# Scores of all four row groups together, and a new order within a tick, in block 0 of a two-block transformer kernel

## The chip, the cores and the metric

The kernel runs on one core of a Trainium2 chip. The metric is the device time of one execution in microseconds. Five engines work from instruction queues of their own, each strictly in order, and meet at semaphores: TensorE (PE, with its weight loads listed apart as PEld), VectorE (DVE), ScalarE (ACT), GpSimd (POOL) and SyncE (SP, which issues transfers here).

## What is computed

Two transformer blocks work on x of 64 batches x 128 tokens x 256 channels, with a context of 64 x 128 x 192 and a conditioning vector. The part that matters here is block 0, whose attention has 16 heads of only 16 channels:

```
def _attn(q, k, v):          # 16 heads of 16 channels
    scores = jnp.einsum('bhnd,bhmd->bhnm', q, k) * HD ** (-0.5)
    p = jax.nn.softmax(scores, axis=-1)
    o = jnp.einsum('bhnm,bhmd->bhnd', p, v)
    return o.transpose(0, 2, 1, 3).reshape(o.shape[0], o.shape[2], D)
h = _ln(x, ln1_w, ln1_b) * (1 + sc1[:, None, :]) + sh1[:, None, :]
qkv = h @ Wqkv + bqkv
x = x + _attn(q, k, v) @ Wos + bos                                     # pass 0
h = _ln(x, ln2_w, ln2_b) * (1 + sc2[:, None, :]) + sh2[:, None, :]
x = x + _attn(h @ Wq + bq, context @ Wk + bk, context @ Wv + bv) @ Woc + boc   # pass 1
```

A feed-forward (pass 2) and block 1 (passes 3 to 5: self attention with 16 heads of 64 channels, cross attention, feed-forward) follow.

## The kernel before

**Work and ticks.** Six passes over the data, each in 16 groups of four batches. `schedule()` writes out by hand, for every stage of every batch, the tick in which it is issued; every engine's program walks the ticks and issues, within a tick, the stages in one fixed order. In passes 0 and 1 ("block 0" in the change's name and here: self and cross attention of the first block, KIND "a") a group takes 16 ticks and a batch four: batch b of a group starts at `tb = tg + 4*b`. Below, "tick 0 to 3" is the tick within a batch's four. The engines aren't synchronised by ticks; a tick is only an order of issue.

**One batch, pass 0 or 1.** fp32 operands are split into a high part (rounded to fp32r) and a low part (the rest), and a product takes three fp32r matmuls (high x high, high x low, low x high; `three`, L607 to L609). q and k are projected for a group of four batches in two units j = 0, 1 each: `q` and `k` on PE (the k projection has a bias matmul more, L709), then `q_high`/`k_high` on ACT (L879; L887, L888) and `q_low`/`k_low` on DVE (L1088; L1095, two operations). The 16 heads lie in four row groups of 32 partitions: row group r serves PSUM bank r (PS[0] to PS[3]), with four heads in each bank.

- `scores0` (PE, L687): in halves. Half h makes banks 2h and 2h+1, as six steps of two matmuls, one in each of two row groups. Half 0 of batch B is issued at tick 2 of batch B-1, half 1 at tick 0 of B.
- `max0` (DVE, L1050): negated maximum of a half's two banks, one tick after its scores.
- `exp0` (ACT, L904): tile u (bank u, four heads), at tick u: four activations with accumulated sums.
- `normal`: reciprocal on DVE (L1063) and product on POOL (L1234), tick u+1.
- `p_turn` (PE, L801): four transposes of the tile, tick u+3. `p_copy` of it out of PSUM, tick u+4: DVE for u < 3 (L1058), ACT for u = 3 (L940).
- `pv0` (PE, L734): probabilities times v, tick 8, that is tick 0 of the batch two later. `high0` (ACT, L895, writes OH) and `low0` (DVE, L1102, writes OL) at tick 9. `out0` (PE, L607 to L609 with OH and OL), tick 10. `res0` (DVE, L1083), tick 11.
- `v` (PE) at tick -3, `v_out` (DVE, L1074) at tick -2.

For a coming group the kernel computes statistics (DVE), normalises (POOL, L1277), turns (`turn`, PE, L823, four parts in four ticks that fall into batch 2 of the current group) and modulates (`hf`, ACT, L951), then splits (`split`, DVE L1010 and POOL L1239). Pass 1 has turns of the context too (`c_turn`, L834), their copies (`c_hf`), splits (`c_split`) and `c_merge` on DVE, on which the k and v projections of that pass wait.

**Order within a tick.** PE: scores0, q, k, v, pv0, out0, p_turn, turn, c_turn. ACT: q_high, k_high, high0, exp0, p_copy, hf, c_hf. DVE: max0, p_copy, normal, v_out, res0, q_low, k_low, low0, statistics, split, c_split, c_merge. POOL: normal, split, c_split, root, norm, bias.

**PSUM.** Banks 0 to 3 hold the scores. Banks 4 to 7 (FOUR) are handed out in turn by `Banks.add`, in the order in which the uses are issued on PE: every projection, v, pv, out0 result, turned tile and turn takes the next of the four and waits until the use four back has been read. A batch without turns has eight uses: pv, p, v, p, out0, p, q or k, p.

The scores wait for the banks at L683: `q.wait_ge(s_exp, 4 * (4 * ga + x.b) + 2 * x.h - 2)`, that is: half 0 waits for the exponentials of tiles 0 and 1 of the batch before, half 1 for tiles 2 and 3.

Of the kernel before, what the change touches and what calls it, by code (L numbers as in the profile page):

```python
# [8 lines left out]
ACT = mybir.ActivationFunctionType  # L9
# [4 lines left out]
NG = NB // G  # L14
# [112 lines left out]
def schedule():  # L127
# [3 lines left out]
    for p, kind in enumerate(KIND):  # L131
        for g in range(NG):
# [51 lines left out]
            if kind == "a":  # L184
                for j in range(2):
                    tq, tk = (tg - 17 + 4 * j, tg - 9 + 4 * j) if (p, g) != (0, 0) else (tg - 17 + j, tg - 15 + j)
                    tq += 2 * ((p, g) == (0, 1))
                    at["q", tq].append((p, g, j))
                    at["q_high", tq + 1].append((p, g, j))
                    at["q_low", tq + 1].append((p, g, j))  # L190
                    at["k", tk].append((p, g, j))
                    at["k_high", tk + 1].append((p, g, j))
                    at["k_low", tk + 1].append((p, g, j))
# [15 lines left out]
            for b in range(G):  # L209
                tb = tg + 4 * b  # L210
                for h in range(2):
                    at["scores0", tb + 2 * h - 2].append(Half(2 * (4 * (NG * p + g) + b) + h, p, g, b, h))
                    at["max0", tb + 2 * h - 1].append(Half(2 * (4 * (NG * p + g) + b) + h, p, g, b, h))
                for stage, tick in (("v", tb - 3), ("v_out", tb - 2), ("pv0", tb + 8), ("high0", tb + 9), ("low0", tb + 9),
                                    ("out0", tb + 10), ("res0", tb + 11)):
                    at[stage, tick].append(Batch(p, g, b))
                for u in range(4):
                    t = Tile(n, p, ATT[p], g, b, u)
                    for stage, lag in (("exp0", 0), ("normal", 1), ("p_turn", 3), ("p_copy", 4)):
                        at[stage, tb + u + lag].append(t)  # L220
                    n += 1
# [19 lines left out]
def build(nc, a, out):  # L241
    ctx = ExitStack()
    with ctx:
# [118 lines left out]
        def xq(p, g):  # L362
            return NG * p + g
# [63 lines left out]
        for tick in ticks:  # L427
            if tick == TM:
                tp.add("modulation", (7,), s_mod, 3)
            for p, g, j in at["q", tick]:  # L430
                tp.add(("q", p, g, j), FOUR, s_al, 2 * xq(p, g) + j + 1)
            for p, g, j in at["k", tick]:
                tp.add(("k", p, g, j), FOUR, s_kbl, 2 * xq(p, g) + j + 1)
# [17 lines left out]
            for t in at["p_turn", tick]:  # L451
                tp.add(("p", t.n), FOUR if t.n < NL0 else THREE, *pt_done(t))
            for stage in ("turn", "c_turn"):
# [146 lines left out]
        def _(e):  # L600
# [66 lines left out]
            for tick in ticks:  # L667
# [8 lines left out]
                for x in at["scores0", tick]:  # L676
# [5 lines left out]
                    q.wait_ge(s_exp, 4 * (4 * ga + x.b) + 2 * x.h - 2)  # L682
                    for c in range(2):  # L683
                        for k, (qt, kt) in enumerate(((AH, KBH), (AH, KBL), (AL, KBH))):
                            for r in (2 * x.h, 2 * x.h + 1):
# [3 lines left out]
                    made.then_inc(s_s0, 1)  # L689

                for p, g, j in at["q", tick]:
                    u, h = h_of(p, g)
                    key = "Wq" if p == 1 else "Wqkv"
                    q.wait_ge(s_hl, 2 * u + 2)
                    q.wait_ge(s_wlo, w_ready[key])
                    q.wait_ge(*tp.free(("q", p, g, j)))
                    project_t(key, 128 * j, h, PS[tp.bank(("q", p, g, j))]).then_inc(s_q, 1)

                for p, g, j in at["k", tick]:
                    u, h = h_of(p, g, p == 1)  # L700
                    key, col0 = ("Wk", 0) if p == 1 else ("Wqkv", 256)
                    q.wait_ge(s_hl, 2 * u + 2)
                    q.wait_ge(s_wlo, w_ready[key])
                    q.wait_ge(s_bk, 2)
                    if p == 1:
                        q.wait_ge(s_hm, cq(p, g) + 1)
                    q.wait_ge(*tp.free(("k", p, g, j)))
                    bank = PS[tp.bank(("k", p, g, j))]
                    e.matmul(bank[:, :], BK[:, p, 128 * j:128 * j + 128], ONES[:, :], start=True, stop=False)  # L709
                    project_t(key, col0 + 128 * j, h, bank, False).then_inc(s_k, 1)  # L710
# [92 lines left out]

                for x in at["out", tick]:
# [57 lines left out]
        def _(e):  # L862
# [9 lines left out]

            for tick in ticks:
                for p, g, j in at["q_high", tick]:
# [21 lines left out]

                for t in at["exp0", tick]:
                    q.wait_ge(s_nm0, t.n // 2 + 1)
                    q.wait_ge(s_t, t.n - NP0 + 1)
                    q.wait_ge(s_nrm, t.n - NP0 + 1)  # L900
                    bank, pr, nm = PS[t.u], PR[npr(t)[0]], NM0[t.n // 2 % 3][:, 4 * (t.n % 2):4 * (t.n % 2) + 4]
                    for h in range(4):
                        r = slice(128 * h, 128 * h + 128)
                        made = e.activation(pr[:, r], bank[:, r], ACT.Exp, bias=nm[:, h:h + 1], accum_out=RL[npr(t)[0]][:, h:h + 1])  # L904
                    made.then_inc(s_exp, 1)
# [59 lines left out]
                for p, g, j in at["up", tick]:  # L965
# [4 lines left out]
                    e.activation(GF[p][f % 3][:, :], PS[tp.bank(("up", p, g, j))][:, :], ACT.Gelu, bias=col(WFF[p][2], j)).then_inc(s_gf, 1)  # L970

# [357 lines left out]
```

## Time and profile before

| | us |
|---|---|
| median of 3 runs (lowest, highest) | 4212.19 (4211.66, 4212.67) |
| the profiled execution, its own time | 4212.79 |
| its span in the profile | 4210.6 |
| PE busy / ACT / DVE / POOL (share of the span) | 4066.8 (97%) / 2751.7 (65%) / 2858.3 (68%) / 2903.7 (69%) |
| L904 exponentials of block 0, 2048 of them | 730.8, and 516.8 for reading their sums |

Times in the trace are microseconds from the span's start, one execution. A group of instructions is named by its line, engine, operation and tiles (written <- read), its shape and count; "idle before" is the time in which that engine had nothing to run ahead of the instruction, with the engine and line that ended the wait. Two starts subtracted give the time that the earlier instruction takes in a queue; the duration in a row is longer where the next one overlaps it. PEclk is the clock that TensorE was granted, 1.00 being 2.4 GHz and 0.50 the lower level.

### The profile page before, as it was taken

The numbers are of one execution on the slowest core, as the hardware profiler recorded it, in microseconds if no ns is written. First come the engines' busy times: TensorE is split into PE (matmuls) and PEld (weight loads), VectorE is DVE, ScalarE is ACT, GpSimd is POOL, SyncE is SP. The second block draws the span as 40 slices with busy tenths as digits, with TensorE's granted clock in tenths as the row PEclk, the third lists the DMA queues.
The fourth block names the chain that finished last, engine by engine and source line by source line (L and its number), as shares of the span: only waits on it lengthen the run. The fifth ranks groups of instructions, "written<-read, shape, count | busy, mean of one in ns | idle before, by whom it ended". The sixth has DMA issues, their size and how long they took to land.

```text
span 4210.6 us, 95756 instructions
## 1 busy us (share of the span) xinstructions
PE 4066.8 (97%) x34870; PEld 3478.2 (83%) x34870; DVE 2858.3 (68%) x6066; ACT 2751.7 (65%) x10788; POOL 2903.7 (69%) x2706
## 2 busy tenths in 40 slices
PE   7999999999999999999999999999999999999999
PEld 6777777777779988888888888888888888888998
DVE  7888888888865556565656565777776767664443
ACT  6999999999953336666666666666666666665333
POOL 5777788888767775666665665666666666666776
PEclk9999999999999999999999999999999999999999
DMA  2101111111111122212121212322222222221110
GB/s 83 32 32 32 32 45 39 43 47 47 50 54 46 61 63 78 82 70 81 71 81 70 80 71 96 105 78 90 85 83 87 83 86 81 89 98 55 41 51 31
DMA packets 230900, 276.64 MB, mean 66 GB/s; under 512 B 38044, under 2 KB 160416, under 8 KB 230432
## 3 DMA queue, kind: packets, MB, share of 16 engines
q1 hardware_dynamic: 230364, 270.51, 19.1%
q8 instruction: 278, 4.55, 0.5%
q14 instruction: 190, 1.56, 0.1%
q10 hardware_dynamic: 68, 0.02, 0.0%
HBM read 85.89 MB, written 50.33 MB: 32 GB/s over the span
## 4 chain that ended last, share of the span: by engine, by line
PE 76%; POOL 9%; DVE 7%; ACT 4%; issue 3%; DMA 0%; ACTq 0%; SPq 0%; DVEq 0%; POOLq 0%
PE BANKS L607 18%; PE BANKS L609 16%; PE BANKS L608 16%; PE BANKS L801 7%; PE BANKS L765 6%; PE BANKS L753 6%; POOL PR L1234 3%; PE BANKS L687 2%; ACT PR L904 2%; POOL Z L1277 2%; PE BANKS L823 2%; POOL HL L1244 1%; DVE WL L1095 1%; POOL X L1291 1%; DVE PT L1058 1%
## 5 line engine op out<-in xcount | busy, mean ns | idle before, releaser
L1234 POOL TENSOR_TENSOR PR<-PR,RL 128x512 f32<-128x512 f32 x1024 | 1067.8, 1047 | 657.7 <-DVE RL L1063 655.8
L920 ACT ACTIVATE PR<-BANKS,NM 128x128 f32<-128x128 f32 x2048 | 730.6, 382 | 443.6 <-DVE NM L1109 439.2
L904 ACT ACTIVATE PR<-BANKS,NM 128x128 f32<-128x128 f32 x2048 | 730.8, 412 | 12.5 <-DVE NM L1050 10.4
L607 PE MATMUL BANKS<-HH,WH 128*128 128x512 f32 x1632 | 689.0, 422 | 5.3 <-POOL HL L1239 2.7
L801 PE MATMUL BANKS<-ID,PR 128*128 128x128 f32 x4096 | 623.7, 275 | 59.3 <-POOL PR L1234 23.5
L1109 DVE TENSOR_REDUCE NM<-BANKS 128x8 f32<-128x1024 f32 x256 | 313.4, 1224 | 488.0 <-PE BANKS L765 488.0
L608 PE MATMUL BANKS<-HL,WH 128*128 128x512 f32 x1632 | 642.6, 394 | 0.0
L609 PE MATMUL BANKS<-HH,WL 128*128 128x512 f32 x1632 | 641.6, 393 | 0.0
L801 PEld LDWEIGHTS BANKS<-ID,PR 128*128 128x128 f32 x4096 | 487.3, 140 | 184.3 <-POOL PR L1234 66.5
L904 ACT ACTIVATION_READ_ACCUMULATOR PR<-BANKS,NM 128x1 f32 x2048 | 516.8, 253 | 0.0
L920 ACT ACTIVATION_READ_ACCUMULATOR PR<-BANKS,NM 128x1 f32 x2048 | 452.6, 221 | 0.0
L1239 POOL TENSOR_TENSOR HL<-HF,HH 128x512 fp32r<-128x512 f32 x192 | 255.4, 1331 | 232.7 <-DVE HH L1011 218.6
L940 ACT ACTIVATE PT<-BANKS 128x512 f32<-128x512 f32 x640 | 405.4, 634 | 10.6 <-PE BANKS L801 1.5
L607 PE MATMUL BANKS<-WH,OH 128*128 128x256 f32 x1280 | 393.6, 307 | 5.7 <-DVE OL L1102 4.7
L607 PEld LDWEIGHTS BANKS<-HH,WH 128*128 128x128 f32 x1632 | 307.1, 188 | 106.8 <-DVE SN L1123 26.4
L951 ACT ACTIVATE HF<-BANKS,MODB,MODS 128x128 f32<-128x128 f32 x768 | 304.2, 482 | 118.8 <-PE BANKS L823 108.0
L1058 DVE COPY PT<-BANKS 128x512 f32<-128x512 f32 x384 | 263.9, 687 | 150.6 <-PE BANKS L801 149.6
L609 PEld LDWEIGHTS BANKS<-HH,WL 128*128 128x128 f32 x1632 | 307.4, 188 | 70.8
L609 PE MATMUL BANKS<-WH,OL 128*128 128x256 f32 x1280 | 358.0, 280 | 0.0
L608 PE MATMUL BANKS<-WL,OH 128*128 128x256 f32 x1280 | 357.3, 279 | 0.0
L911 ACT ACTIVATE OH<-BANKS 128x512 fp32r<-128x512 f32 x256 | 153.6, 600 | 301.2 <-PE BANKS L753 300.7
L1123 DVE TENSOR_TENSOR SN<-BANKS,ROPE 128x512 f32<-128x512 f32 x512 | 348.8, 681 | 1.6 <-DMA SW<-SN 1.5
(132 smaller groups left out, 10742.0 us busy)
## 6 DMA issues: line engine op xcount, KB each, us to landing
SW<-SN SPq DMA_DIRECT2D x1024, 128.0 KB, 2.1
x_scratch<-X SPq DMA_DIRECT2D x80, 512.0 KB, 3.1
X<-x_scratch SPq DMA_DIRECT2D x80, 512.0 KB, 4.0
CX<-in_ctx SPq DMA_DIRECT2D x32, 384.0 KB, 4.1
X<-in_x SPq DMA_DIRECT2D x16, 512.0 KB, 3.8
out<-X SPq DMA_DIRECT2D x16, 512.0 KB, 2.9
CX<-in_ctx SPq DMA_DIRECT2D x32, 128.0 KB, 4.3
STG<-in_L_xcond_W SPq DMA_DIRECT2D x4, 512.0 KB, 4.9
```

The source lines that it names most:

```text
L607: e.matmul(o, lh, rh, start=first and i == 0, stop=False)
L608: e.matmul(o, lh, rl, start=False, stop=False)
L609: made = e.matmul(o, ll, rh, start=False, stop=last and i == n - 1)
L801: made = e.transpose(bank[:, 128 * h:128 * h + 128], PR[npr(t)[0]][:, 128 * h:128 * h + 128], ID[:, :])
L904: made = e.activation(pr[:, r], bank[:, r], ACT.Exp, bias=nm[:, h:h + 1], accum_out=RL[npr(t)[0]][:, h:h + 1])
L920: made = e.activation(pr[:, r], bank[:, r], ACT.Exp, bias=nm[:, h:h + 1], accum_out=RL[npr(t)[0]][:, h:h + 1])
L940: e.activation(PT[npt(t)[0]][:, :], PS[tp.bank(("p", t.n))][:, :], ACT.Copy).then_inc(s_pt_a, 1)
L951: made = e.activation(HF[u % 2][:, x.c, r], bank[:, r], ACT.Identity, bias=MODB[:, s, x.c, bb:bb + 1], scale=MODS[:, s, x.c, bb:bb + 1])
L1058: e.tensor_copy(PT[npt(t)[0]][:, :], PS[tp.bank(("p", t.n))][:, :]).then_inc(s_pt_d, 1)
L1109: e.tensor_reduce(NM[x.i % 2][:, :], BANKS[:, 2:4, :].rearrange("p e (h k) -> p (e h) k", h=4), AX, ALU.max, negate=True).then_inc(s_nm, 1)
L1123: e.tensor_tensor(SN[r % 2][:, :].rearrange("p (b t) -> p b t", b=G), src, sn, ALU.mult).then_inc(s_rt, 1)
L1234: e.tensor_tensor(p3, p3, RL[npr(t)[0]][:, :].unsqueeze(2).broadcast_to([128, 4, 128]), ALU.mult).then_inc(s_nrm, 1)
```

## The change

1. Scores of a batch are made in one go: one PE stage at tick 0 of the batch, six steps of four matmuls, one in each row group. It waits for all exponentials of the batch before.
2. The maxima of its halves are at ticks 0 and 1 (they were at -1 and 1).
3. The q and k projections are issued one tick earlier (tick 2 in place of tick 3) and stand behind p_turn in the tick, for PE and for the order of the banks; the high parts are a tick earlier too (tick 3), the low parts stay where they were (tick 0).
4. On ACT, the exponentials of tiles 1, 2 and 3 are first in their tick, that of tile 0 is last in its tick, behind the modulation copies.

The diff, cut only where a moved piece stands twice:

```diff
--- before.py
+++ after.py
@@ -183,14 +183,14 @@
                 continue
             if kind == "a":
                 for j in range(2):
-                    tq, tk = (tg - 17 + 4 * j, tg - 9 + 4 * j) if (p, g) != (0, 0) else (tg - 17 + j, tg - 15 + j)
-                    tq += 2 * ((p, g) == (0, 1))
+                    tq, tk, late = (tg - 18 + 4 * j, tg - 10 + 4 * j, 2) if (p, g) != (0, 0) else (tg - 17 + j, tg - 15 + j, 1)
+                    tq += 4 * ((p, g) == (0, 1))
                     at["q", tq].append((p, g, j))
                     at["q_high", tq + 1].append((p, g, j))
-                    at["q_low", tq + 1].append((p, g, j))
+                    at["q_low", tq + late].append((p, g, j))
                     at["k", tk].append((p, g, j))
                     at["k_high", tk + 1].append((p, g, j))
-                    at["k_low", tk + 1].append((p, g, j))
+                    at["k_low", tk + late].append((p, g, j))
             if kind == "b":
                 for j in range(8):
                     x = Unit(unit, p, g, j)
@@ -208,9 +208,9 @@
                 continue
             for b in range(G):
                 tb = tg + 4 * b
+                at["scores0", tb].append(Batch(p, g, b))
                 for h in range(2):
-                    at["scores0", tb + 2 * h - 2].append(Half(2 * (4 * (NG * p + g) + b) + h, p, g, b, h))
-                    at["max0", tb + 2 * h - 1].append(Half(2 * (4 * (NG * p + g) + b) + h, p, g, b, h))
+                    at["max0", tb + h].append(Half(2 * (4 * (NG * p + g) + b) + h, p, g, b, h))
                 for stage, tick in (("v", tb - 3), ("v_out", tb - 2), ("pv0", tb + 8), ("high0", tb + 9), ("low0", tb + 9),
                                     ("out0", tb + 10), ("res0", tb + 11)):
                     at[stage, tick].append(Batch(p, g, b))
@@ -427,10 +427,6 @@
         for tick in ticks:
             if tick == TM:
                 tp.add("modulation", (7,), s_mod, 3)
-            for p, g, j in at["q", tick]:
-                tp.add(("q", p, g, j), FOUR, s_al, 2 * xq(p, g) + j + 1)
-            for p, g, j in at["k", tick]:
-                tp.add(("k", p, g, j), FOUR, s_kbl, 2 * xq(p, g) + j + 1)
             for x in at["v", tick]:
                 tp.add(("v", x), FOUR, s_vd, 4 * xq(x.p, x.g) + x.b + 1)
             for x in at["pv0", tick]:
@@ -450,6 +446,10 @@
                 tp.add(("k1", x.i), THREE if x.i > 1 else TWO, s_rt, 2 * x.i + 2)
             for t in at["p_turn", tick]:
                 tp.add(("p", t.n), FOUR if t.n < NL0 else THREE, *pt_done(t))
+            for p, g, j in at["q", tick]:
+                tp.add(("q", p, g, j), FOUR, s_al, 2 * xq(p, g) + j + 1)
+            for p, g, j in at["k", tick]:
+                tp.add(("k", p, g, j), FOUR, s_kbl, 2 * xq(p, g) + j + 1)
             for stage in ("turn", "c_turn"):
                 for x in at[stage, tick]:
                     hparts[stage, x] = len(hparts)
@@ -679,35 +679,14 @@
                     q.wait_ge(s_mod, 2)
                     q.wait_ge(s_al, 2 * ga + 2)
                     q.wait_ge(s_kbl, 2 * ga + 2)
-                    q.wait_ge(s_exp, 4 * (4 * ga + x.b) + 2 * x.h - 2)
+                    q.wait_ge(s_exp, 4 * (4 * ga + x.b))
                     for c in range(2):
                         for k, (qt, kt) in enumerate(((AH, KBH), (AH, KBL), (AL, KBH))):
-                            for r in (2 * x.h, 2 * x.h + 1):
+                            for r in range(4):
                                 rows = slice(32 * r, 32 * r + 32)
                                 made = e.matmul(PS[r][:, 256 * c:256 * c + 256].rearrange("p (e n) -> p e n", e=2), qt[ga % 2][rows, c, s],
                                                 kt[ga % 2][rows, c, :, s], start=k == 0, stop=k == 2)
-                    made.then_inc(s_s0, 1)
-
-                for p, g, j in at["q", tick]:
-                    u, h = h_of(p, g)
-                    key = "Wq" if p == 1 else "Wqkv"
-                    q.wait_ge(s_hl, 2 * u + 2)
-                    q.wait_ge(s_wlo, w_ready[key])
-                    q.wait_ge(*tp.free(("q", p, g, j)))
-                    project_t(key, 128 * j, h, PS[tp.bank(("q", p, g, j))]).then_inc(s_q, 1)
-
-                for p, g, j in at["k", tick]:
-                    u, h = h_of(p, g, p == 1)
-                    key, col0 = ("Wk", 0) if p == 1 else ("Wqkv", 256)
-                    q.wait_ge(s_hl, 2 * u + 2)
-                    q.wait_ge(s_wlo, w_ready[key])
-                    q.wait_ge(s_bk, 2)
-                    if p == 1:
-                        q.wait_ge(s_hm, cq(p, g) + 1)
-                    q.wait_ge(*tp.free(("k", p, g, j)))
-                    bank = PS[tp.bank(("k", p, g, j))]
-                    e.matmul(bank[:, :], BK[:, p, 128 * j:128 * j + 128], ONES[:, :], start=True, stop=False)
-                    project_t(key, col0 + 128 * j, h, bank, False).then_inc(s_k, 1)
+                    made.then_inc(s_s0, 2)
 
                 for x in at["v", tick]:
                     u, h = h_of(x.p, x.g, x.p == 1)
@@ -800,6 +779,27 @@
                     for h in range(4):
                         made = e.transpose(bank[:, 128 * h:128 * h + 128], PR[npr(t)[0]][:, 128 * h:128 * h + 128], ID[:, :])
                     made.then_inc(s_t, 1)
+
+                for p, g, j in at["q", tick]:
...
+                for p, g, j in at["k", tick]:
...
 
                 for x in at["out", tick]:
                     key, k = ("co" if x.p == 4 else "so"), x.i % 2
@@ -870,7 +870,20 @@
                 for i in range(2):
                     e.dma_start(CROWB[r + 1:r + 2, 64 * i:64 * i + 64], a[key][128:CD].unsqueeze(0)).then_inc(s_crows, 16)
 
+            def exponentials(tiles):
+                for t in tiles:
+                    q.wait_ge(s_nm0, t.n // 2 + 1)
+                    q.wait_ge(s_t, t.n - NP0 + 1)
+                    q.wait_ge(s_nrm, t.n - NP0 + 1)
+                    bank, pr, nm = PS[t.u], PR[npr(t)[0]], NM0[t.n // 2 % 3][:, 4 * (t.n % 2):4 * (t.n % 2) + 4]
+                    for h in range(4):
+                        r = slice(128 * h, 128 * h + 128)
+                        made = e.activation(pr[:, r], bank[:, r], ACT.Exp, bias=nm[:, h:h + 1], accum_out=RL[npr(t)[0]][:, h:h + 1])
+                    made.then_inc(s_exp, 1)
+
             for tick in ticks:
+                exponentials([t for t in at["exp0", tick] if t.u])
+
                 for p, g, j in at["q_high", tick]:
                     ga = xq(p, g)
                     q.wait_ge(s_q, 2 * ga + j + 1)
@@ -893,16 +906,6 @@
                     q.wait_ge(s_mods, 5)
                     q.wait_ge(s_y, vi - 2)
                     e.activation(OH[vi % 3][:, :, :], PS[tp.bank(("pv", x))][:, 0:256].rearrange("p (c t) -> p c t", c=2), ACT.Copy).then_inc(s_oh, 1)
-
-                for t in at["exp0", tick]:
...
                 for x in at["low", tick]:
                     q.wait_ge(s_pv, x.i + 1)
@@ -968,6 +971,8 @@
                     q.wait_ge(s_gl, f - 2)
                     q.wait_ge(*((s_s0, 16 * NG) if p == 2 else (s_s, 16 * NG)))
                     e.activation(GF[p][f % 3][:, :], PS[tp.bank(("up", p, g, j))][:, :], ACT.Gelu, bias=col(WFF[p][2], j)).then_inc(s_gf, 1)
+
+                exponentials([t for t in at["exp0", tick] if not t.u])
 
                 for w, key, c in at["w_split", tick]:
                     q.wait_ge(s_win[w % NSTG], arrived[w])
```

## Rows read from the trace of the kernel before

**Rows 1.** Windows: busy time of each engine, granted clock, DMA share, GB/s.
```profile
core 0: us, PE busy (x) PEld busy (x) DVE busy (x) ACT busy (x) POOL busy (x), PEclk, DMA share, GB/s
200.00:400.00 200.00, 187.72 (x2122) 158.61 (x2123) 169.15 (x389) 185.64 (x858) 158.62 (x160) 1.00 0.10 33
```

**Rows 2.** Timeline of PE: score matmuls a group apart (start, us, engine, line).
```profile
479.00 0.38 PE L687 MATMUL BANKS<-WH,AH 32*128 32x256 f32 x2 [0.16 <-ACT PR L904]
...
513.88 0.39 PE L687 MATMUL BANKS<-WH,AH 32*128 32x256 f32 x2 [0.16 <-ACT PR L904]
...
860.51 0.38 PE L687 MATMUL BANKS<-WH,AH 32*128 32x256 f32 x2 [0.56 <-ACT PR L904]
...
897.11 0.38 PE L687 MATMUL BANKS<-WH,AH 32*128 32x256 f32 x2 [0.58 <-ACT PR L904]
```

**Rows 3.** Timeline of PE, 502 to 510 us.
```profile
502.04 0.39 PE L687 MATMUL BANKS<-WH,AH 32*128 32x256 f32 x2
502.26 0.28 PE L687 MATMUL BANKS<-WL,AH 32*128 32x256 f32 x2
...
502.94 1.08 PE L734 MATMUL BANKS<-PT,V 128*32 128x128 f32 x32
503.95 0.66 PE L801 MATMUL BANKS<-ID,PR 128*128 128x128 f32 x4
...
505.92 0.39 PE L687 MATMUL BANKS<-WH,AH 32*128 32x256 f32 x2 [0.16 <-ACT PR L904]
...
506.82 0.38 PE L607 MATMUL BANKS<-WH,OH 128*128 128x256 f32 x1
...
507.63 0.60 PE L801 MATMUL BANKS<-ID,PR 128*128 128x128 f32 x4
507.99 0.48 PE L607 MATMUL BANKS<-HH,WH 128*128 128x512 f32 x1
...
509.46 0.60 PE L801 MATMUL BANKS<-ID,PR 128*128 128x128 f32 x4
509.99 0.39 PE L687 MATMUL BANKS<-WH,AH 32*128 32x256 f32 x2
```

**Rows 4.** Timeline of ACT, 504 to 519 us.
```profile
504.08 0.39 ACT L895 ACTIVATE OH<-BANKS 128x256 fp32r<-128x256 f32 x1 [0.29 <-PE BANKS L734]
504.36 0.36 ACT L904 ACTIVATE PR<-BANKS,NM 128x128 f32<-128x128 f32 x1
...
505.74 0.39 ACT L904 ACTIVATE PR<-BANKS,NM 128x128 f32<-128x128 f32 x1
...
517.83 0.69 ACT L887 ACTIVATE WH<-BANKS,MASK 128x512 fp32r<-128x512 f32 x1 [0.72 <-PE BANKS L609]
...
518.98 0.37 ACT L904 ACTIVATE PR<-BANKS,NM 128x128 f32<-128x128 f32 x1
```

**Rows 5.** Timeline of DVE, 504 to 520 us.
```profile
504.03 1.19 DVE L1050 TENSOR_REDUCE NM<-BANKS 128x8 f32<-128x1024 f32 x1
505.13 0.68 DVE L1058 COPY PT<-BANKS 128x512 f32<-128x512 f32 x1
...
505.82 0.40 DVE L1102 TENSOR_TENSOR OL<-BANKS,OH 128x256 fp32r<-128x256 f32 x1
506.13 0.42 DVE L1142 BATCH_NORM_STATS2 ST<-X 128x6 f32<-128x256 f32 x1
...
506.68 0.67 DVE L1058 COPY PT<-BANKS 128x512 f32<-128x512 f32 x1
...
507.35 0.46 DVE L1074 TENSOR_TENSOR V<-BANKS,TB 128x128 f32<-128x128 f32 x2
...
519.13 1.41 DVE L1095 SCALAR_TENSOR_TENSOR WL<-BANKS,MASK,WH 128x512 fp32r<-128x512 f32 x2
```

**Rows 6.** Waits of ACT, 0 to 1400 us (waited for, total us, times, longest).
```profile
ACT AH L879 <- PE BANKS L609: 44.1, 63, 4.7
```

**Rows 7.** Windows of PE near the end of block 0 (busy, instructions, granted clock).
```profile
1172.20:1175.60 3.40, 1.60 (x16) 1.00 0.89 251
1175.60:1182.40 6.80, 6.14 (x30) 0.50 0.20 66
```

More of the change, by code:

```diff
@@ L802, in _ @@
                     made.then_inc(s_t, 1)
+                for p, g, j in at["q", tick]:
+                    u, h = h_of(p, g)
+                    key = "Wq" if p == 1 else "Wqkv"
+                    q.wait_ge(s_hl, 2 * u + 2)
+                    q.wait_ge(s_wlo, w_ready[key])
+                    q.wait_ge(*tp.free(("q", p, g, j)))
+                    project_t(key, 128 * j, h, PS[tp.bank(("q", p, g, j))]).then_inc(s_q, 1)
+                for p, g, j in at["k", tick]:
+                    u, h = h_of(p, g, p == 1)
+                    key, col0 = ("Wk", 0) if p == 1 else ("Wqkv", 256)
+                    q.wait_ge(s_hl, 2 * u + 2)
+                    q.wait_ge(s_wlo, w_ready[key])
+                    q.wait_ge(s_bk, 2)
+                    if p == 1:
+                        q.wait_ge(s_hm, cq(p, g) + 1)
+                    q.wait_ge(*tp.free(("k", p, g, j)))
+                    bank = PS[tp.bank(("k", p, g, j))]
+                    e.matmul(bank[:, :], BK[:, p, 128 * j:128 * j + 128], ONES[:, :], start=True, stop=False)
+                    project_t(key, col0 + 128 * j, h, bank, False).then_inc(s_k, 1)
                 for x in at["out", tick]:
@@ L895, in _ @@
                     e.activation(OH[vi % 3][:, :, :], PS[tp.bank(("pv", x))][:, 0:256].rearrange("p (c t) -> p c t", c=2), ACT.Copy).then_inc(s_oh, 1)
-                for t in at["exp0", tick]:
[L898 to L905, printed above, removed]
                 for x in at["low", tick]:
```

## The prediction

> **What bounds the kernel now.** I read the windows first. In block 0 PE is busy 188 of 200 us and ACT 186 of 200, at full clock [rows 1]: two engines at about 93%, DVE not far behind, so a microsecond saved on one need not be one off the time. A difference under 0.2% (8 us) can hardly be measured here. Then the period: a group is four batches of four ticks, and the same score instruction comes again after 513.88 - 479.00 = 34.88 us in self attention and 897.11 - 860.51 = 36.60 us in cross attention [rows 2]. Each pass has 16 groups, so block 0 is 16 x 71.48 = 1144 us of the 4210.6. All the rest of the kernel is left alone.
>
> The PE timeline [rows 3] reads without a gap: half scores 0.90 us, out0 0.81, transposes of a tile 0.36 ahead of a projection, q 1.47, transposes 0.53 ahead of scores, half scores 0.90, pv0 1.01; v has out0's six matmuls of 256 columns, some 0.8. PE is the bound here because two half score stages keep ACT fed: exponentials of one half run while the other half's scores are made.
>
> **Part 1, scores in one go.** Six steps of four matmuls replace twelve steps of two. A step of two is (502.94 - 502.04 - 0.22)/6, about 0.115 us [rows 3], the 0.22 being the first step's. A step of four isn't in the trace: at least 0.115 if four row groups overlap as two do, at most 0.23 if only two do. The nearest row is pv0: 32 small matmuls issued in 1.01 us, 0.032 each, so four take 0.126. I take that: results after 1.00 us from the first score, occupancy about 0.95, a saving of some 0.85 us of PE a batch, 109 us in all. The Trainium skill (TensorE: Matmul & The Clock Gate, part 3) gives 3.07 times for four row groups, not four times; by that a step would be 0.15, and 0.15 us a batch (19 us) would be added to the sum. No row here shows it.
>
> **What is lost with it.** One go needs all four score banks, so scores of batch B wait for the last exponential of B-1, and exp of B cannot begin before scores and the first maximum. Nothing overlaps these any more. From the first score s, exp u=0 starts at 1.00 + 0.03 + 1.19 (maximum, [rows 5]) + 0.03 = s+2.25. A tile of exponentials is 505.74 - 504.36 = 1.38 us [rows 4], so even ACT alone needs 2.25 + 4 x 1.38 + 0.28 (OH) = 8.1 us a batch plus modulation copies, against 8.72 on the average before.
>
> **Part 2, exponentials first.** The decisive edit. At tick 1 of a batch ACT now runs exp u=1 and only then copies OH of batch B-2. DVE makes OL from OH behind the second maximum and a PT copy, and PE has out0(B-2) at the head of tick 2, behind it p_turn, the q or k projection (moved here), p_turn of tick 3, then the next scores. That is a closed loop:
> s + 2.25 + 2.76 (two tiles) + 0.03 + 0.39 (OH) + 0.03 + 0.40 (OL) + 0.03 = out0 at s+5.89; + 0.81 + 0.36 + projection + 0.53. A q projection is 1.47 [rows 3]; a k projection has one matmul more, 1.71. So 9.06 for q, **9.3 for k**. PE's own work is only about 6.8; it idles from about s+4.7, after v and p_turn, to s+5.9.
>
> **DVE in the same loop.** DVE can't start the batch until the first maximum (free at s+2.13). Then PT copy and reciprocal 0.69, q_low 0.70 or k_low 1.41 (two operations of that kind), perhaps statistics 0.55, second maximum 1.10, PT copy and reciprocal 0.69, OL 0.40 [rows 5]. PSUM banks 4 to 7 rotate in the order of the uses, so each use waits for the release of the one four back: v waits for q_low/k_low, the q or k projection for v_out, and with turns in between a p_turn for OL. v_out is now in the projection's own tick, no longer one ahead. The four batches of a self attention group:
> - Batch 0 (q_low, statistics, q): OL at 6.26 (2.13 + 0.69 + 0.70 + 0.55 + 1.10 + 0.69 + 0.40); then statistics 0.55, PT copy, reciprocal, v_out 0.46 until 7.88; q from 7.9; + 1.47 + 0.53 = 9.9.
> - Batch 1 (q_low, k): 9.3 as above.
> - Batch 2 (k_low, k, four turns): OL 6.42, p_turn 0.42, turn 0.2, out0 0.81; v_out only at 8.2 frees the next p_turn; k from 8.6 to 10.3. The last turn needs the bank that ACT's PT copy frees, and that copy is now queued behind k_high (1.15, [rows 4]): 10.4 + 1.15 + 0.67 = 12.2; turn and scores follow: 12.6.
> - Batch 3 (k_low, q, a split): pv0 waits for k_low until 4.2, so p_turn, PT copy and OL slip to 7.1; a split (of a PT copy's size) 0.60, PT copy, v_out until 8.7; q: 10.8.
> Sum 42.6 against 34.88: +7.7. In cross attention batch 0 carries context turns (10.5), in batch 1 the k projection now shares the tick of c_merge and waits for it (9.6), batches 2 and 3 about 12.4 and 10.7: 43.2 against 36.60, +6.6. Together 16 x 14.3 = **+229 us**.
>
> **The other moves.** q_high and k_high a tick earlier take ACT's wait for the projection away (44.1 us in all for AH, [rows 6]), but the loop above does not pass through q_high. Only k_high ahead of the PT copy counts, and stands in batch 2. No DMA is added or moved past another; SP's queue is as before. POOL (80% busy) gets the same work over a longer period: nothing. The first fill and the border to the feed-forward change by a batch or so: under 10 us, none taken.
>
> **The clock.** A stretch with PE busy 1.60 of 3.40 us was followed by 6.8 us at 0.50, the 1.2 GHz level; before it the clock was 1.00 [rows 7]. In the forecast PE is as idle as that at the head of batch 3 (turn wait, then scores, then pv0 waiting) and nearly so elsewhere. An estimate of the price: PE's work from out0 to the next scores, 3.2 us, doubles if all of it falls in such a stretch, and nothing is lost where the clock stays. The two stretches with waits of that size are in one batch of four; I take 2.0 us of the 3.2 in that batch in every group that is hit, and every second group hit, as the row's case is right at what the forecast has: 1.0 us a group, 32 us.
>
> **Sum.** 4212.8 (the profiled execution, 0.6 above the median; span 4210.6) + 229 + 32 = 4474; the same against the median. I say **4475**.
>
> **Rivals.**
> - *Faster:* the OH loop doesn't bind, and only ACT's own round remains. 16 x [4 x 8.1 + 1.3 for the turns' copies = 33.7, and 34.9 in cross attention] is 46 us under 1144: 4166. For it: PE and ACT do idle on each other now [rows 6], and PE loses 0.85 us of work a batch. It decides if OL is ready within 5 us of the scores; against it, OH stands behind two whole tiles of exponentials. 0.10. A middle case near no change: 0.04.
> - *Plain loop only:* the waits of bank rotation fall away and every batch costs 9.3 at most: 128 x 9.3 = 1190, +46, 4259; with half of them, 4350. 0.14.
> - *Row groups don't overlap beyond two* (the change does not do what it says): results 0.6 us later in the loop, 128 x 0.6 = +77: 4550. The matmuls of a pair are seen to overlap, and pv0's, which sit side by side by columns, too [rows 3]. 0.09.
> - *Clock half in every batch 2 and 3 and in some others:* 3.2 us in each of 64, +205 in place of 32: 4647. 0.13.
> - The forecast itself, 4400 to 4540: 0.50.
>
> The range is 4255 to 4650: it takes in all but the rivals at or under the time of before (0.14 together) and the edges of the rest. Chances: slower 0.86, same 0.04, faster 0.10.
>
> **What would show it.** Right: out0's first matmul, or the transposes ahead of it, waits for DVE's OL, over 0.5 us in most batches, the top wait of PE in block 0; the period is 41 to 45 us a group; PE and ACT both under 85% busy there; ACT's exp waits for the maximum (NM) once a batch; PE's busy time in the score line about half of before; the granted clock below 1.00 in block 0. Wrong: a period under 36 us, or scores that come directly behind the last exponential with PE idle only there (then ACT's round is the bound), or score steps over 0.2 us.

## The result, and the profile after

The changed kernel takes **4538.2 us** (median of four, 4534.1 to 4542.6) against 4211.9 before: ratio 1.0774, 95% interval 1.0762 to 1.0787, 326 us slower. The forecast was 4475 us, in a range of 4255 to 4650.

The windows answer to [rows 1]: PE was busy 188 of 200 us and is busy 148, ACT 186 and is 142, and the granted clock, which was 1.00, is 0.89.

```profile
200.00:400.00 200.00, 147.62 (x1637) 121.85 (x1634) 128.31 (x292) 142.26 (x654) 122.31 (x124) 0.89 0.09 28
```

No engine is near its limit, and every engine does the work of before, PE less. In the groups of score matmuls (line, shape, count, then busy us, mean ns, idle before) the busy time is 87.7 + 74.0 + 73.9 = 235.6 us, where it was 171.4 + 143.2 + 143.1 = 458. The first three rows are the kernel before, the others the changed one:

```profile
L687 PE MATMUL BANKS<-WH,AH 32*128 32x256 f32 x1024 | 171.4, 331 | 28.6 <-ACT PR L904 28.4
L687 PE MATMUL BANKS<-WL,AH 32*128 32x256 f32 x1024 | 143.2, 277 | 0.0
L687 PE MATMUL BANKS<-WH,AL 32*128 32x256 f32 x1024 | 143.1, 276 | 0.0
...
L687 PE MATMUL BANKS<-WH,AH 32*128 32x256 f32 x1024 | 87.7, 332 | 0.1
L687 PE MATMUL BANKS<-WL,AH 32*128 32x256 f32 x1024 | 74.0, 278 | 0.0
L687 PE MATMUL BANKS<-WH,AL 32*128 32x256 f32 x1024 | 73.9, 277 | 0.0
```

The saved work does not shorten anything, since waits take its place and more. The waits of block 0 after the change (who waits, for whom: total us, times, longest), PE's six largest, one of ACT's and two of DVE's, and last DVE's wait for scores in the kernel before:

```profile
PE BANKS L713 <- DVE WL L1100: 99.2, 30, 3.3
PE BANKS L607 <- DVE OL L1107: 59.0, 50, 3.0
PE BANKS L780 <- DVE OL L1107: 53.8, 46, 1.4
PE BANKS L607 <- DVE AL L1093: 46.3, 44, 1.1
PE BANKS L823 <- DVE WL L1100: 38.4, 32, 1.2
PE BANKS L823 <- ACT PT L943: 35.6, 30, 1.2
...
ACT PR L881 <- DVE NM L1055: 178.7, 129, 7.0
...
DVE NM L1055 <- PE BANKS L687: 368.1, 123, 4.9
DVE PT L1063 <- PE BANKS L780: 96.4, 100, 1.9
...
DVE NM L1050 <- PE BANKS L687: 1.1, 1, 1.1
```

L713 is pv0, L780 p_turn, L823 a turn, L607 the first matmul of v, out0 or a projection; WL is the result of k_low, the line at AL is q_low, NM is the maximum. Before, DVE waited for scores once in all of block 0; now it waits 123 times, once a batch, and ACT waits for the maximum once a batch behind it.

The score instruction of a group's batch 0 answers to [rows 2]: 512.79 - 465.31 = 47.48 us for one self attention group, 557.47 - 512.79 = 44.68 for the next, in place of 34.88.

```profile
465.31 0.39 PE L687 MATMUL BANKS<-WH,AH 32*128 32x256 f32 x4
...
512.79 0.39 PE L687 MATMUL BANKS<-WH,AH 32*128 32x256 f32 x4
...
557.47 0.39 PE L687 MATMUL BANKS<-WH,AH 32*128 32x256 f32 x4
```

Batch 0 of the second of these groups, at full clock, shows the loop from one score (512.79) to the next (522.69). The timelines of PE, then DVE, then ACT answer to [rows 3 to 5]:

```profile
512.79 0.39 PE L687 MATMUL BANKS<-WH,AH 32*128 32x256 f32 x4
513.01 0.29 PE L687 MATMUL BANKS<-WL,AH 32*128 32x256 f32 x4
...
513.48 0.28 PE L687 MATMUL BANKS<-WH,AL 32*128 32x256 f32 x4
513.70 1.08 PE L713 MATMUL BANKS<-PT,V 128*32 128x128 f32 x32
...
516.42 0.39 PE L607 MATMUL BANKS<-WH,HH 128*128 128x256 f32 x1 [1.06 <-DVE AL L1093]
...
519.07 0.38 PE L607 MATMUL BANKS<-WH,OH 128*128 128x256 f32 x1 [1.24 <-DVE OL L1107]
...
520.67 0.50 PE L607 MATMUL BANKS<-HH,WH 128*128 128x512 f32 x1 [0.18 <-DVE V L1079]
...
522.69 0.39 PE L687 MATMUL BANKS<-WH,AH 32*128 32x256 f32 x4
```

```profile
513.82 1.23 DVE L1055 TENSOR_REDUCE NM<-BANKS 128x8 f32<-128x1024 f32 x1 [1.70 <-PE BANKS L687]
514.96 0.68 DVE L1063 COPY PT<-BANKS 128x512 f32<-128x512 f32 x1
...
516.83 1.19 DVE L1055 TENSOR_REDUCE NM<-BANKS 128x8 f32<-128x1024 f32 x1
...
518.62 0.39 DVE L1107 TENSOR_TENSOR OL<-BANKS,OH 128x256 fp32r<-128x256 f32 x1
...
520.15 0.46 DVE L1079 TENSOR_TENSOR V<-BANKS,TB 128x128 f32<-128x128 f32 x2
```

```profile
515.08 0.37 ACT L881 ACTIVATE PR<-BANKS,NM 128x128 f32<-128x128 f32 x1 [1.44 <-DVE NM L1055]
...
517.83 0.42 ACT L908 ACTIVATE OH<-BANKS 128x256 fp32r<-128x256 f32 x1
```

Counted from s = 512.79: maximum +1.03, exponentials +2.29, OH +5.04, OL +5.83, out0 +6.28, q projection +7.88, next scores +9.90. DVE works without a gap from 513.82 to 521.0 and then stands still for 2.7 us, until the next scores. Over 200 to 1100 us it is busy 590 of 900 us, 66%: most of its idle time is this wait for scores (368.1 us), the rest mainly the wait for the transposes that it copies (96.4 us). (The wait for exponentials ahead of the scores is line 682 of the kernel before, not 683 as the part ahead of the forecast has it.)

### The profile page after: what moved, and what is told of

It is laid out like the page before. It is cut to its first block, busy times and chain, and to the rows that moved or that the text cites. A ratio compares the mean times of both kernels' runs of the same rounds, so it can differ in the third digit from the quotient of the medians.

```text
span 4540.4 us, 95756 instructions
## 1 busy us (share of the span) xinstructions
PE 4085.2 (90%) x34870; PEld 3478.9 (77%) x34870; DVE 2856.7 (63%) x6066; ACT 2761.0 (61%) x10788; POOL 2903.2 (64%) x2706
## 4 chain that ended last, share of the span: by engine, by line
PE 74%; DVE 14%; POOL 5%; ACT 4%; issue 3%; DMA 0%; ACTq 0%; SPq 0%; DVEq 0%; POOLq 0%
PE BANKS L607 17%; PE BANKS L608 15%; PE BANKS L609 15%; PE BANKS L780 8%; PE BANKS L744 6%; PE BANKS L732 5%; DVE NM L1055 5%; PE BANKS L687 2%; DVE PT L1063 2%; ACT PR L881 2%; DVE WL L1100 2%; POOL PR L1239 2%; PE BANKS L823 2%; PE BANKS L713 1%; POOL HL L1249 1%
## 5 line engine op out<-in xcount | busy, mean ns | idle before, releaser
L780 PE MATMUL BANKS<-ID,PR 128*128 128x128 f32 x4096 | 663.6, 288 | 82.5 <-DVE OL L1107 53.8
L607 PE MATMUL BANKS<-HH,WH 128*128 128x512 f32 x1632 | 695.4, 426 | 11.5 <-POOL HL L1244 3.7
L780 PEld LDWEIGHTS BANKS<-ID,PR 128*128 128x128 f32 x4096 | 515.8, 147 | 209.9 <-issue 127.4
L1114 DVE TENSOR_REDUCE NM<-BANKS 128x8 f32<-128x1024 f32 x256 | 313.3, 1224 | 486.7 <-PE BANKS L744 486.7
L1055 DVE TENSOR_REDUCE NM<-BANKS 128x8 f32<-128x1024 f32 x256 | 311.4, 1217 | 368.1 <-PE BANKS L687 368.1
L881 ACT ACTIVATION_READ_ACCUMULATOR PR<-BANKS,NM 128x1 f32 x2048 | 480.2, 234 | 0.0
L607 PE MATMUL BANKS<-WH,OH 128*128 128x256 f32 x1280 | 401.5, 314 | 60.7 <-DVE OL L1107 60.1
L923 ACT ACTIVATION_READ_ACCUMULATOR PR<-BANKS,NM 128x1 f32 x2048 | 452.6, 221 | 0.0
L607 PEld LDWEIGHTS BANKS<-HH,WH 128*128 128x128 f32 x1632 | 310.9, 190 | 121.2 <-DVE SN L1128 26.5
L943 ACT ACTIVATE PT<-BANKS 128x512 f32<-128x512 f32 x640 | 392.7, 614 | 11.3 <-PE BANKS L780 2.2
L954 ACT ACTIVATE HF<-BANKS,MODB,MODS 128x128 f32<-128x128 f32 x768 | 294.8, 469 | 120.6 <-PE BANKS L823 109.9
L608 PEld LDWEIGHTS BANKS<-HL,WH 128*128 128x128 f32 x1632 | 311.7, 191 | 40.2
```

The source lines that it names most:

```text
L607: e.matmul(o, lh, rh, start=first and i == 0, stop=False)
L608: e.matmul(o, lh, rl, start=False, stop=False)
L780: made = e.transpose(bank[:, 128 * h:128 * h + 128], PR[npr(t)[0]][:, 128 * h:128 * h + 128], ID[:, :])
L943: e.activation(PT[npt(t)[0]][:, :], PS[tp.bank(("p", t.n))][:, :], ACT.Copy).then_inc(s_pt_a, 1)
L954: made = e.activation(HF[u % 2][:, x.c, r], bank[:, r], ACT.Identity, bias=MODB[:, s, x.c, bb:bb + 1], scale=MODS[:, s, x.c, bb:bb + 1])
L1055: e.tensor_reduce(NM0[x.i % 3][:, :], BANKS[:, 2 * x.h:2 * x.h + 2, :].rearrange("p r (h k) -> p (r h) k", h=4), AX, ALU.max, negate=True) ...
```

## Experiments

The edits below are shortened: a remark in them stands for the rest of an edit.

**One edit alone, and one undone.** e1 is the kernel before with

```diff
-    at["scores0", tb + 2 * h - 2]; at["max0", tb + 2 * h - 1]
+    at["scores0", tb] (both halves, four row groups a step); at["max0", tb + h]
```

> The kernel before with the scores in one go and the maxima at ticks 0 and 1, but projections and exponentials in their old places. Theory (closed loop: scores, first maximum, DVE's queue of copies, low parts and second maximum, OL, out0, projection, next scores): the loop is the same without the other two edits, since PE's order out0, p_turn, projection, p_turn is the same; only batch 2's turn no longer waits behind k_high (1.2 us in each of 32 groups) and v_out and c_merge are a tick ahead of the projection (some 0.5 us a group): 4470 to 4500 us, over 80% of the loss. Rival (OH behind the exponentials is what costs): with OH ahead of them OL comes with the end of pv0 and the loss is mostly gone: 4300 us or less.

Measured 4460.0 us, 1.0591 times the kernel before (95% interval 1.0573 to 1.0609): +248 us, 10 us under the theory's range and 160 over the rival's. OH stands ahead of the exponentials here and the loss is there all the same. e2 moves only the projections, with their high parts:

```diff
-    tq, tk = tg - 17 + 4 * j, tg - 9 + 4 * j      # low parts at tq + 1; ahead of v in the tick
+    tq, tk = tg - 18 + 4 * j, tg - 10 + 4 * j     # low parts at tq + 2; behind p_turn
```

> The kernel before with only the q and k projections a tick earlier and behind the transposes. Theory: PE's order is nearly that of before; the last turn of batch 2 waits for a PT copy behind k_high on ACT, the cross attention's k waits for c_merge: 4215 to 4260 us. Rival (projections are moved at no cost): 4212 us within 5.

Measured 4506.9 us, 1.0703 (1.0681 to 1.0725). Both expectations failed by over 240 us. The waits of PE and ACT in block 0 say why:

```profile
PE BANKS L687 <- ACT PR L904: 191.8, 133, 4.2
PE BANKS L823 <- ACT PT L940: 77.6, 30, 2.6
...
ACT AH L879 <- PE BANKS L609: 169.8, 64, 5.6
```

q_high (AH, and k_high like it) a tick earlier stands ahead of the tick's exponential, waits there for the projection that PE makes in the same round, and the scores then wait for the exponential. I had expected this of e4, which undoes the exponentials' move in the changed kernel, and overlooked it for the kernel before. e3 moves only the exponentials:

```diff
+    exponentials([t for t in at["exp0", tick] if t.u])        # first in ACT's tick
     q_high, k_high, high0
-    exp0
     p_copy, hf, c_hf, up
+    exponentials([t for t in at["exp0", tick] if not t.u])    # last
```

> The kernel before with only the exponentials of tiles 1 to 3 first in ACT's tick and tile 0's last. Theory: scores in halves keep the loop through the first maximum open, so OH 1.4 us later still meets DVE's slot for OL; PE stays the bound: 4190 to 4230 us. Rival (OH behind exponentials costs by itself): out0 waits for OL some 0.5 to 1 us a batch: 4280 to 4340 us.

Measured 4219.1 us, 1.0017 (1.0007 to 1.0026): 7 us slower, as the theory had it. With scores in halves, OH behind a tile of exponentials costs next to nothing.

> The changed kernel with the exponentials back in their old place (behind q_high, k_high and OH), scores in one go and projections moved. Theory: ACT's last exponential of a batch then waits for the projection of the same round (ready 8.4 to 8.8 us after the scores), for q_high or k_high (0.6 or 1.15) and takes 1.38, before the next scores: 1 to 2 us a batch more, 4650 to 4800 us; that is what this edit was needed for. Rival (OH behind the exponentials is what costs): faster than the changed kernel by over 100 us, 4300 to 4430 us.

Measured 4797.9 us, 1.1391 (1.1374 to 1.1408), at the upper end of the theory's range; the rival's sign is wrong.

**Pairs of edits.** e5 has both orders of the change and keeps the scores in halves; e6 has one go and the exponentials' order, and the projections of before.

> The kernel before (scores in halves) with both other edits, projections moved and exponentials first. The run with projections alone lost 295 us, which theory now puts on ACT: q_high and k_high, ahead of the last exponential in the tick, make it wait for the projection of the same round. With exponentials ahead of them that goes. Theory: 4225 to 4300 us, the rest being the turn behind k_high and k behind c_merge; the changed kernel's loss is then the one go. Rival (the projections' new place is bad by itself, through v_out and the banks): 4400 us or more.

> The changed kernel with the projections back in their old place. Theory: as the run with one go alone (4460), plus OH behind two tiles in the batches without k_low (some 0.2 us each): 4460 to 4490 us, so OH's place is worth under 30 us. Rival (OH behind the exponentials is what costs): 4530 us or more.

e5: 4270.4 us, 1.014 (1.0124 to 1.0155). e6: 4460.8 us, 1.0593 (1.0576 to 1.0611), the same as e1. Both as the theory expected. The largest sums of PE's waits in e5 are the turn that waits for ACT's PT copy behind k_high, and p_turn that waits for POOL:

```profile
PE BANKS L823 <- ACT PT L943: 35.6, 30, 1.2
PE BANKS L780 <- POOL PR L1239: 29.4, 44, 1.0
```

Put together, in us over the kernel before:

| | exponentials in old place | exponentials first |
|---|---|---|
| halves, projections of before | 0 | +7 (e3) |
| halves, projections moved | +295 (e2) | +60 (e5) |
| one go, projections of before | +248 (e1) | +250 (e6) |
| one go, projections moved | +586 (e4) | +326 (the change) |

One go, with the maxima at their new ticks, costs 248 us by itself, 243 (250 - 7) with the exponentials first, and 266 (326 - 60) to 291 (586 - 295) where the projections are moved. The projections' move costs 53 (60 - 7) to 76 (326 - 250) where the exponentials stand ahead of it. The exponentials' own move costs 2 to 7, and with the projections moved it saves 235 (295 - 60) to 260 (586 - 326). Part of these sums is a lower granted clock, which the runs don't separate from the waits that cause it. The trace's time at half clock is 44 us in the kernel before, 41 in e3, 51 in e5, 255 in e2, 323 in e1, 307 in e6, 333 in the changed kernel and 624 in e4.

**Do four row groups overlap?** e7 makes the same 24 matmuls in twelve steps:

```diff
+    for pair in ((0, 1), (2, 3)):
         for c ...: for k ...:
-            for r in range(4):
+            for r in pair:
```

> The changed kernel with the same 24 score matmuls in twelve steps of two row groups. Theory (four row groups do overlap, and the scores lie on the loop): results and next instruction some 0.7 us later, 128 x 0.7 = 90 us more: 4610 to 4650 us, steps of 0.12 us in both. Rival (row groups overlap only by twos): as the changed kernel, 4538 us within 15.

Measured 4597.9 us, 1.0919 (1.0903 to 1.0935): 60 us more than the changed kernel, so twelve steps are slower, if by 12 us less than the lower end of the theory's range; the rival's 4538 us within 15 is missed as well. The timeline of PE in e7 (from 500.51) beside that of the changed kernel above (from 512.79):

```profile
500.51 0.39 PE L688 MATMUL BANKS<-WH,AH 32*128 32x256 f32 x2
...
500.87 0.39 PE L688 MATMUL BANKS<-WH,AH 32*128 32x256 f32 x4
...
501.32 0.28 PE L688 MATMUL BANKS<-WH,AH 32*128 32x256 f32 x2
...
501.56 0.28 PE L688 MATMUL BANKS<-WH,AL 32*128 32x256 f32 x2
```

In the changed kernel a step of four takes (513.48 - 513.01)/4 = 0.118 us, and a step of two in e7 (501.56 - 501.32)/2 = 0.12: four row groups overlap as two do. In e7 the second pair starts at 500.87, 0.36 us behind the first, and runs beside it. The row of 500.87 has four matmuls, the second pair's first step and the first pair's fourth. The last step starts 1.05 us after the first, against 0.69 in the changed kernel. The period of a batch 1 is 9.71 us, against 9.36, so nearly all of these 0.36 us are paid.

**OH, OL, or DVE's whole queue?** e8 puts `high0` first on ACT and `low0` first on DVE, ahead of the exponentials and the maxima.

> The changed kernel with OH ahead of the exponentials on ACT and OL ahead of the second maximum on DVE. Theory (it is DVE's whole queue behind the first maximum, up to v_out, that the projection waits for): OL comes over 1 us earlier, but v_out does not, since the queue is as long; and in batch 3 the late pv0 holds the second maximum: 4500 to 4570 us. Rival (OL alone is the wait that counts): 1.3 us a batch less, 4370 us.

Measured 4540.5 us, 1.0782 (1.0766 to 1.0798), 2 us from the changed kernel: the theory's range. The waits for OL are gone from the head of PE's list, others have their place, and ACT now waits 2.5 us for the late pv0 in batch 3:

```profile
PE BANKS L713 <- DVE WL L1106: 99.2, 30, 3.3
PE BANKS L607 <- DVE AL L1099: 46.2, 44, 1.1
...
ACT OH L890 <- PE BANKS L713: 74.2, 30, 2.5
```

The equal time is a balance, and the theory held only in part. In the self attention groups with half clock in batch 3 alone, batches 0 and 1 take 10.0 and 9.7 us (9.9 and 9.4 in the changed kernel), batch 2 takes 12.0 (12.9) and batch 3 takes 13.4 (12.5). An earlier OL does save 0.9 us in batch 2, and the late pv0 takes it back in batch 3.

e9 and e10 put one idle product on DVE (its output is read by nobody; 0.68 us), in tick 0 of 120 of the 128 batches, into the changed kernel and the kernel before:

```diff
+    e.tensor_tensor(PAD[:, 0:512], ROPE, ROPE, ALU.mult)    # ahead of p_copy in tick 0
```

> The changed kernel with one idle product of 128 x 512 on DVE (about 0.6 us, nobody reads it) in tick 0 of nearly every batch of block 0, between the two maxima. Theory (DVE's queue from the first maximum to OL and v_out is a link of the loop): the full 0.6 us in batches 0, 2 and 3, some 0.3 in batch 1, since OH alone is nearly as late there: 16 x 2 x 2.1 = 60 to 75 us more, 4595 to 4620 us. Rival (DVE has slack, being busy 65% in block 0): 4540 us within 15.

> The kernel before with the same idle product in tick 0 of nearly every batch, behind nothing but the maximum of that tick's place. Theory: scores in halves leave DVE idle 1.3 us a batch (mostly ahead of the PT copy) that takes it up, apart from batches with k_low: 0 to 30 us more, 4212 to 4242 us. Rival (DVE is as close to the bound here): 60 us or more, 4272 us.

e9: 4660.9 us, 1.1064 (1.1049 to 1.1079), 123 more than the changed kernel: 1.02 us for each 0.68 us of work. e10: 4234.8 us, 1.0053 (1.0037 to 1.0068), 22 more: 0.19 us each. DVE's queue is a link of the loop with one go and mostly hidden with halves. Batches of e9 in which the clock stayed at full speed show it without the clock. The product takes 0.60 us from its start to that of the next operation. Batch 0 of self attention takes 496.34 - 485.84 = 10.50 us where it took 9.90, batch 1 9.74 (9.36), batch 2 13.52 (12.91), and batch 0 of cross attention 11.32 (10.72): the whole 0.60, except in batch 1, of which 0.3 was expected, OH alone being nearly as late there.

```profile
485.84 0.39 PE L689 MATMUL BANKS<-WH,AH 32*128 32x256 f32 x4
...
496.34 0.39 PE L689 MATMUL BANKS<-WH,AH 32*128 32x256 f32 x4
```

That e9 exceeds the expected 75 us goes with the clock, which is at half for 511 us of the trace and for 333 in the changed kernel; the windows of 200 to 1100 us, PE and so on, in the changed kernel and then e9, have 0.90 and 0.86:

```profile
200.00:1100.00 900.00, 655.74 (x7238) 541.56 (x7234) 590.18 (x1346) 649.27 (x2944) 561.14 (x564) 0.90 0.10 30
```

```profile
200.00:1100.00 900.00, 635.12 (x6758) 524.18 (x6756) 598.24 (x1327) 607.95 (x2734) 523.63 (x523) 0.86 0.09 27
```

**The clock.** e11 gives PE idle matmuls where it waits:

```diff
     made = project(... v ...)
+    for _ in range(6):                                      # into columns of v's bank that nobody reads
+        made = e.matmul(PS[...][:, 256:512], wview(WH, key)[:, 0, 0:128], HH[h][:, 0, 0:256], start=True, stop=True)
```

> The changed kernel with six idle matmuls of 128 x 256 (0.7 us of PE in all) behind each v projection, where PE waits for OL anyway. Theory (the granted clock falls because PE idles there, and groups whose batches 0 and 1 fall are 2.8 us longer): fewer falls in batches 0 and 1, batch 3 falls as before, since it waits ahead of v: 20 to 45 us less, 4493 to 4518 us, under 280 us at half clock where it was 333. Rival (the clock is no cost; the added work only delays v_out and the next transposes): 4540 to 4580 us.

Measured 4525.9 us, 1.0745 (1.073 to 1.076): 12 us faster than the changed kernel with 0.7 us more PE work in each batch. The granted clock over 200 to 1100 us is 0.94, where it was 0.90, and the self attention groups whose batches 0 and 1 took 11.0 and 10.8 us now take 9.9 and 9.4 throughout. The time at half clock fell from 333 to 201 us, further than expected, and the gain is less than the 20 to 45 expected: batch 3 of about half of the groups became slower (13.1 to 13.9 us where 12.5 to 12.7 was usual).

**A try at something faster than both.**

> A try at a kernel faster than both: the kernel before, scores in halves, projections in their old place, with OH first in ACT's tick, then the exponentials of tiles 1 to 3, then q_high and k_high. Theory: PE has under 0.2 us of waits left in a plain batch, so at most 10 to 20 us: 4190 to 4215 us. Rival (as the run with exponentials first alone): 4219 us.

Measured 4212.2 us, 0.9999 (0.999 to 1.0007): no difference. The expected range held, but the gain that it allowed did not come. Beside e3, which differs from it only by the place of OH, it is 7 us less: with halves, the 7 us of the exponentials' move are OH's place. Nothing here beats the kernel before.

## Why the prediction was right, and what it mis-sized

**The loop held, to a tenth in batch 0.** Of its steps: maximum at +1.03 (measured 1.03), exponentials +2.25 (2.29), OL in batch 0 at 6.26 (its end at 518.62 + 0.39, +6.22), v_out until 7.88, for which the forecast's own terms add up to 7.96, and q at 7.9 (7.88), next scores 9.9 (9.90). Batch 1 was forecast at 9.3 (9.36 in the undisturbed groups), batch 2 at 12.6 (12.9), with its turn waiting for ACT's PT copy 1.2 us (1.2, 30 times). In cross attention 10.5, 9.6 and 12.4 stand against 10.7, 9.8 and 12.7. The range of 4255 to 4650 holds nearly every slower outcome, so that the time lies in it says little; these steps say more.

**Two signs did not come.** PE's top wait was to be the one for OL. It is the one for k_low: 99.2 + 38.4 = 137.6 us against 59.0 + 53.8 = 112.8. The forecast had k_low's waits, in batches 2 and 3, but not as the largest. And the period is 44.7 to 47.6 us in self and 45.3 to 47.1 in cross attention, above the 41 to 45 that were given, by the clock (below).

**"The decisive edit" was named wrongly (part 2).** The forecast gave that title to the exponentials' place and let OH close the loop. By e1 and e6 the place of OH is worth 1 us in one go. In their groups with the least half clock the self attention batches take 9.9, 9.13, 12.0 and 10.5 us with OH ahead of the exponentials and 9.9, 9.36, 12.0 and 10.5 behind them: DVE's queue brings OL at the same time or later in all batches but batch 1, as the forecast's own sum for batches 0, 2 and 3 already had it. What decides is the one go: everything on DVE starts from the first maximum, and its copies, low parts, second maximum, OL and v_out then follow in series ahead of the projection. e9 and e10 show that DVE's queue is in the loop, and e1 alone gives 248 of the 326 us. The exponentials' place is needed all the same, for another reason than OH: without it (e4) the last exponential waits behind q_high and k_high, for 260 us more.

**What was mis-sized is the clock's term.** The forecast took 2.0 us in batch 3 of every second group. In the changed kernel batch 3 runs from 500.07 to 512.79, 12.72 us, and the windows over it, the row of 496.80 being the end of batch 2, are

```profile
496.80:500.20 3.40, 2.21 (x17) 1.00 0.00 0
500.20:503.60 3.40, 0.84 (x24) 0.85 0.00 0
503.60:507.00 3.40, 2.65 (x37) 0.50 0.02 5
507.00:510.40 3.40, 3.40 (x22) 0.65 0.00 0
510.40:513.80 3.40, 3.23 (x41) 1.00 0.01 2
```

PE was busy 0.84 of 3.40 us while pv0 waited 3.31 us for k_low, and the clock fell within that wait; then it is at 0.50, the 1.2 GHz level, through pv0, v and p_turn:

```profile
504.35 1.93 PE L713 MATMUL BANKS<-PT,V 128*32 128x128 f32 x32 [3.31 <-DVE WL L1100]
506.21 1.12 PE L780 MATMUL BANKS<-ID,PR 128*128 128x128 f32 x4
506.98 0.56 PE L607 MATMUL BANKS<-WH,HH 128*128 128x256 f32 x1
...
508.41 1.05 PE L780 MATMUL BANKS<-ID,PR 128*128 128x128 f32 x4
```

pv0, p_turn and v take 508.41 - 504.35 = 4.06 us there. At full clock they are 1.01 + 0.36 + 0.82 = 2.2 (pv0 and v in batch 0 above, p_turn in [rows 3]). So the clock costs some 1.9 us in this batch, an estimate, since no batch 3 of the changed kernel with its waits ran at full clock. (In e6 one did, in 10.47 us, but there pv0 runs ahead of the wait for k_low, which p_turn has.) The price of 2.0 us was about right, and a batch 3 without it comes to 10.5 to 10.8 us (most take 12.5, some 12.7), where 10.8 was forecast. But it falls due in every group: 1.0 us a group more than taken.

To this comes half clock in batches 0 and 1 of every second self attention group (11.02 + 10.84 in place of 9.9 + 9.36, 2.6 us), and in about every second group of cross attention batch 0 takes 11.9 in place of 10.7, or batch 2 13.7 in place of 12.7. That is 16 x (1.0 + 1.3) + 16 x (1.0 + 0.6), about 62 us, worked out from these periods. Groups of the changed kernel in which these batches had full clock show the shorter times, and so does e11 in all of them. The clock's term is then 94 us, not 32. That 62 agrees so well with the missing 63 (4538 - 4475) is partly luck: without the clock the periods would be 44.7 - 2.0 - 34.9 = 7.8 us longer than before in self and 45.7 - 2.0 - 36.6 = 7.1 in cross attention, 16 x 14.9 = 238 in place of the forecast's 229, and the first and last groups, which are not of that period, take some 6 us off.

**The other moves.** q_high a tick earlier was said to take away ACT's wait for the projection. It grew: ACT's wait for it [rows 6] was 44.1 us, and is 96.3. ACT reaches q_high early, with nothing behind it that PE then waits for. Behind k_high the PT copy comes late not only for the turn: pv0 of batch 2 waits 0.5 us for it, 30 times, which the forecast did not have. The whole of the projections' move came to 53 us with halves and 76 with one go, of which the turn's wait for ACT's PT copy is 35.6 us in e5 and in the changed kernel. What c_merge and v_out have of the rest no run separates. PE's one go saved 222 us of busy time on PE and none of the kernel's.

**Rivals.** "Faster" was wrong because the loop through DVE, not ACT's round of 8.1 us, is the longest. "Plain loop only" fell by batches 2 and 3, at 12.9 and 12.5 us with the waits of the bank rotation in them. "Row groups don't overlap beyond two" fell by the step of 0.118 us and by e7. The clock rival was half right: the clock is at half in every batch 3 and in some others, but seldom in batch 2, and a batch pays about 2 us, not 3.2. From the 3.07 times that the Trainium skill (TensorE: Matmul & The Clock Gate, part 3) gives for four row groups at 512 columns, a step of four would be an estimated 0.15 us. It takes 0.118, as a step of two does, so for the 256 columns of this kernel the measurement decides against carrying that figure over.

## What to carry to other kernels

Before two half stages are merged to save an engine's time, follow the ring of waits through every engine's queue: halves that look wasteful may be the double buffer that lets the engines overlap. Its length is the sum of what each engine issues in order between the links, whatever their busy shares, and a queue of cheap operations behind one late wait (here DVE's, busy 66%) counts in full: 0.60 us of idle work in it made a batch 0.60 us longer. And when a stage moves earlier, ask what stands behind its consumer in the consumer's queue: a wait moved ahead of the last exponential cost 295 us, and a new order of the stages behind it took 235 of them back.

## What the runs showed of the hardware

- A wait of PE can be paid twice. After 3.31 us of waiting PE came back at a granted clock of 0.50, which stayed for some 7 us and cost the batch an estimated 2 us. Shorter waits do it too: a batch 0 with waits of 1.06 and 1.24 us ran in 9.9 us in one group and with 3.4 us at half clock, in 11.0, in the next. Idle matmuls in such waits took the time at half clock from 333 to 201 us and made the kernel 12 us faster although nobody reads their result.
- Six steps of four score matmuls, one in each row group, took no longer a step than steps of two: 0.118 us, against 0.12 in e7.
- Two chains of matmuls in different row groups ran beside each other even when issued one behind the other (e7): the second began 0.36 us after the first, 0.33 us before the first chain's last step (at 500.51 + 0.69 = 501.20), and before the first chain's fourth. So PE's queue isn't quite as strictly in order as the section on the chip has it: across row groups, a later matmul started ahead of an earlier one.
